# A selective scan whose first four states a unit are weighted and summed by GpSimd before one turn, with B rows in a ring of six quarters

## The reference

```
hidden, gate = split(x @ W_in)                       # 512 channels each
hs   = silu(conv(hidden) + conv_bias)                # 4 taps along the sequence
dt, B, C = split(hs @ W_x, [128, 128 + 16])
dts  = softplus(dt @ W_dt + b_dt)
state[n] = exp(dts * A[n]) * state[n] + dts * B[n] * hs      # 16 states n, 256 steps
y    = (sum over n of C[n] * state[n] + hs * D) * silu(gate)
out  = y @ W_out
```

## Time and profile before

| what | value |
|---|---|
| median of 3 runs | 560.07 us (559.85 to 563.25) |
| profiled execution, its own time | 561.63 us |
| its span | 559.8 us |
| instructions | 10,385 |
| mean granted clock of TensorE | 0.938 of full |
| DMA | 64.16 MB, queue busy 35.9% of 16 engines |

### The profile page before, as it was taken

The page is one execution under the profiler, slowest core; times in us unless marked ns, Lnnn a source line. Parts: engine busy times, 40 slices in busy tenths (PEclk is TensorE's granted clock), DMA queues, the critical chain, the costliest instruction groups (busy, mean ns, idle before and its releaser), DMA issues.

```text
span 559.8 us, 10385 instructions
## 1 busy us (share of the span) xinstructions
PE 497.2 (89%) x3304; PEld 435.6 (78%) x3304; DVE 472.0 (84%) x1053; ACT 365.0 (65%) x877; POOL 318.8 (57%) x465
## 2 busy tenths in 40 slices
PE   4857376868876999999999999999999999999996
PEld 3535264637765988888898998998999999999985
DVE  1399999979999899999999999999889997745451
ACT  2489967578957866689958797974976481350210
POOL 1056669853688677548946676795649443334042
PEclk9798568679996999999999999999999999999999
DMA  7612920003472454021530566436055206553000
GB/s 192 213 63 74 380 76 2 0 0 104 134 260 90 133 177 134 30 76 58 164 120 5 155 190 220 132 89 194 2 161 170 87 15 211 175 164 105 11 11 9
DMA packets 26517, 64.16 MB, mean 115 GB/s; under 512 B 4512, under 2 KB 8352, under 8 KB 26080
## 3 DMA queue, kind: packets, MB, share of 16 engines
q1 hardware_dynamic: 26464, 63.50, 35.9%
HBM read 62.38 MB, written 1.11 MB: 113 GB/s over the span
## 4 chain that ended last, share of the span: by engine, by line
PE 64%; DVE 16%; issue 8%; POOL 5%; ACT 4%; DMA 2%; SPq 0%; DVEq 0%; POOLq 0%; ACTq 0%
PE work L616 40%; PE work L670 13%; PE h_bank L592 6%; DVE acc L1197 5%; POOL dbu L545 4%; DVE st L1181 3%; PE work L592 2%; DVE m L1144 1%; PE h_bank L693 1%; ACT dA L964 1%; DVE wk L1148 1%; DMA b_rows<-b_dram 1%; DVE du L1113 1%; DVE bst L1016 1%; PE work L749 1%
## 5 line engine op out<-in xcount | busy, mean ns | idle before, releaser
L545 POOL TENSOR_TENSOR dbu<-du,b_rows 128x512 f32<-128x512 f32 x128 | 163.4, 1278 | 30.5 <-DVE du L1133 21.0
L964 ACT ACTIVATE dA<-dts,a_neg 128x127 f32<-128x127 f32 x512 | 156.6, 355 | 21.1 <-DVE st L1181 20.0
L1181 DVE TENSOR_TENSOR_SCAN st<-dA,dbu 128x512 f32<-128x512 f32 x128 | 155.1, 1214 | 3.3 <-ACT dA L964 2.7
L592 PE MATMUL h_bank<-ident,st 128*128 128x128 f32 x512 | 85.8, 302 | 32.8 <-DVE acc L1197 21.8
L616 PE MATMUL work<-xsT,stream 128*128 128x128 f32 x896 | 110.0, 278 | 0.8 <-DVE du L1113 0.7
L616 PEld LDWEIGHTS work<-xsT,stream 128*128 128x128 f32 x896 | 105.9, 194 | 2.8 <-DVE du L1113 0.9
L592 PEld LDWEIGHTS h_bank<-ident,st 128*128 128x128 f32 x512 | 66.3, 156 | 47.9 <-DVE st L1181 38.9
L1197 DVE SCALAR_TENSOR_TENSOR acc<-h_bank,c_cols,acc 128x512 f32<-128x512 f32 x128 | 93.2, 728 | 7.4 <-issue 3.4
L567 POOL TENSOR_TENSOR hb<-hb,wbt 128x512 f32<-128x512 f32 (+2 forms) x48 | 55.2, 1153 | 54.0 <-ACT wbt L836 36.3
L491 POOL TENSOR_SCALAR var<-mv 128x1 f32<-128x1 f32 x56 | 13.1, 234 | 83.5 <-DVE mv L1017 83.1
L670 PE MATMUL work<-stream,hb 128*128 128x256 f32 x224 | 53.6, 381 | 0.0
(11 more groups left out here) (157 smaller groups left out, 795.0 us busy)
## 6 DMA issues: line engine op xcount, KB each, us to landing
stream<-in_stream SPq DMA_DIRECT2D x48, 512.0 KB, 3.8
stream<-in_stream SPq DMA_DIRECT2D x48, 384.0 KB, 3.8
b_rows<-b_dram SPq DMA_DIRECT2D x32, 256.0 KB, 4.5
wg<-in_wg SPq DMA_DIRECT2D x1, 1280.0 KB, 7.7
wu<-in_wu SPq DMA_DIRECT2D x1, 1280.0 KB, 10.3
wd<-in_wd SPq DMA_DIRECT2D x1, 1280.0 KB, 12.9
xT<-in_xT SPq DMA_DIRECT2D x4, 256.0 KB, 4.2
out<-row SPq DMA_DIRECT2D x8, 128.0 KB, 2.1
```

Of the source, the lines that this page charges most:

```text
L545: gp.tensor_tensor(tile, du[:, batch % 2, :, lo:hi], b_rows[:, b % 2, k:k + 1, :].to_broadcast([P, ET, P]), ALU.mult).then_inc(s["dbu_read ...
L592: return nc.tensor.transpose(dst, src, ident[:, :])
L964: last = A(dA[i % DA_RING][:, t, 1:P], dts[:, batch % 2, t, lo + 1:hi], ACT.Exp, scale=a_neg[:, t, k:k + 1])
L1181: V.tensor_tensor_scan(st[:, i % ST_RING].rearrange("p t l -> p (t l)"), dA[i % DA_RING].rearrange("p t l -> p (t l)"), dbu[:, i % DBU_RIN ...
```

## The change

- The first EARLY = 4 states of a unit aren't turned one by one. ScalarE writes skip * hs to a tile `early` (four scaled copies, 128x128 each). GpSimd multiplies each of the first four states by its row of C, spread over the partitions (c_rows), into `weighted`, and adds it to `early`. It does so at its scan steps 4 to 7: the weighting ahead of the B product of that step, the addition behind it. A scan tile of these states is free once it is weighted (`taken`).
- TensorE turns states 4 to 15 and, one step later than the last of them, `early` as a sum. ScalarE reads the first of these banks into acc with the scale C[4]; VectorE adds states 5 to 15 as before, and the sum by a plain addition. skip_diag and its products are gone.
- Rows 16 to 19 of b_t (the first four of C) are stored to DRAM with those of B, and spread_c reads them back, one more transfer of 256 KB a unit.
- b_rows is a ring of six quarters (4 states each), and each transfer waits for its own quarter; the SP string orders them one by one among the stream chunks.
- A new load part 7 holds batch 0 of ctxT, wqT, wkT and gam and stands third; the rest of ctxT stays in part 4.
- sq shares the tile of tf, with a wait for the product that read it.
- All ORDER strings and BANK are new. ORDER's parts below are the first lines of three of them.

```diff
 DA_RING, DBU_RING, ST_RING = 2, 4, 4
+B_RING = 6
+EARLY = 4
...
-        "s": [... for step in [("skip", g, 0)] + [("scan", g, k) for k in range(N + LAG)]],
+        "s": [... for step in [("skip", g, 0)] + [("scan", g, k) for k in range(N + LAG + 1)]],
-        "l": [("load", part, 0) for part in range(7)],
+        "l": [("load", part, 0) for part in (0, 1, 7, 2, 3, 4, 5, 6)],
-        "r": [("spread", u, 0) for u in range(U)],
+        "r": [("spread", u, k) for u in range(U) for k in (0, B_PARTS, *range(1, B_PARTS))],
...
     "pe": [
-        "ppappappppsmpsssppssspssssssssmsssssmmssaaaaaaaaaaaaasassmspppssssmmsssmssaspsssmmmmppfssfmmmssmsfffsfsspsfmmf",
+        "ppapppapppmpppmssssssspsssssspppssaaaaaaaaaaaaasasassmmmsssssssssssssmmssmsmmmmpssssppmmmsssssssspssaaaaaaaaaa",
...
     "dve": [
-        "ppaaaaappappppsspssaasssssasasasassssssaassssssssssmmmmmssmsssssssmmppppppmpasmsssmssssffmmmmmsffaaassmafffaas",
+        "ppaaappppppssspsaasasaasasaassaaasssssasssasaaassssaasaasssammmmmassssmssssmmsmsssmssspppppppsmsassasaasassasss",
...
     "pool": [
-        "ssssssssssssssspppppppppppppssssssssmmmsssssssssmmsssspssssssmmmsmmmmmmssssssmmfffffffssssmmmsppppppfffmmfffhs",
+        "ssssssssssssspppppppppppppsssssssssssshmmmssssssmmssssssmmmpsssssssmmssmmmmssssssssssssssssmmsppppppsmmmssmmsm",
...
             def spread_b(u, i):
                 b, lt = divmod(u, LT)
                 n, q = N // B_PARTS, B_PARTS * u + i
                 if i == 0:
                     sp.wait_ge(b_stored[b % 2], 16 * LT * (b // 2 + 1))
+                if q >= B_RING:
+                    sp.wait_ge(s["dbu_ready"], n * (q - B_RING + 1))
+                src = b_dram[b, lt, i * n:(i + 1) * n, :].partition_broadcast(P)
+                sp.dma_start(b_rows[:, q % B_RING], src).then_inc(b_loaded[q % B_RING], 16)
+            def spread_c(u):
+                b, lt = divmod(u, LT)
+                sp.wait_ge(b_stored[b % 2], 16 * LT * (b // 2 + 1))
+                if u >= 2:
+                    sp.wait_ge(s["taken"], EARLY * (u - 1))
+                sp.dma_start(c_rows[:, u % 2], b_dram[b, lt, N:N + EARLY, :].partition_broadcast(P))
...
-            for t in range(ET):
-                last = gp.tensor_scalar(skip_diag[:, t, :], ident[:, :], skip[:, t:t + 1], None, ALU.mult)
...
+                    n = k - ST_RING
+                    if 0 <= n < EARLY:
+                        if n == 0:
+                            pool.wait_ge(c_loaded[b % 2], 16 * (b // 2 + 1))
+                        if b or n:
+                            pool.wait_ge(s["summed"], EARLY * b + n)
+                        if hands_on(b):
+                            pool.wait_ge(s["carry_ready"], hands.index(b) * N + n + 1)
+                        gp.tensor_tensor(weighted[:, :, :], st[:, (i - ST_RING) % ST_RING],
+                                         c_rows[:, b % 2, n:n + 1, :].to_broadcast([P, ET, P]), ALU.mult)\
+                            .then_inc(s["taken"], 1)
...
+                if stage == "scan" and 0 <= k - ST_RING < EARLY:
+                    n = k - ST_RING
+                    pool.wait_ge(s["taken"], EARLY * b + n + 1)
+                    if n == 0:
+                        pool.wait_ge(s["skipped"], b + 1)
+                    gp.tensor_tensor(early[:, :, :], early[:, :, :], weighted[:, :, :], ALU.add).then_inc(s["summed"], 1)
...
+            def turn_sum(g):
+                pe.wait_ge(s["summed"], EARLY * (g + 1))
+                for j in range(widths[g]):
+                    t = claim_h(turned_at[g, N, j])
                     for e in range(ET):
+                        last = transpose(t[:, e * P:(e + 1) * P], early[:, e, j * P:(j + 1) * P])
...
-                if stage == "scan" and 0 < k <= N:
+                if stage == "scan" and EARLY < k <= N:
                     turn_state(b, k - 1)
+                if stage == "scan" and k == N + 1:
+                    turn_sum(b)
...
                 if stage == "skip":
+                    batch, (lo, hi) = GROUPS[b][0], columns(b)
+                    if b == 0:
+                        act.wait_ge(loaded[3], part_size[3])
+                    else:
+                        act.wait_ge(s["h_full"], turned_at[b - 1, N, 0] + 1)
+                    act.wait_ge(s["hs_ready"], batch + 1)
+                    for t in range(ET):
+                        last = A(early[:, t, :], hs[:, batch % 2, t, lo:hi], ACT.Copy, scale=skip[:, t:t + 1])
+                    last.then_inc(s["skipped"], 1)
+                if stage == "scan" and k == EARLY + LAG:
...
                         act.wait_ge(s["h_full"], at + 1)
+                        A(acc[:, u % ACC_RING, :], h_bank[at % H_BANKS][:, :], ACT.Copy,
+                          scale=c_cols[:, batch % 2, u % LT, EARLY:EARLY + 1]).then_inc(s["first_read"], 1)
...
                         if i >= ST_RING:
                             before, n = divmod(i - ST_RING, N)
+                            if n < EARLY:
+                                dve.wait_ge(s["taken"], EARLY * before + n + 1)
+                            else:
+                                dve.wait_ge(s["h_full"], turned_at[before, n, widths[before] - 1] + 1)
...
-                    if k >= LAG:
-                        n = k - LAG
+                    n = k - LAG
+                    if n > EARLY:
...
+                            if n < N:
+                                last = V.scalar_tensor_tensor(out=sums, in0=turned_state, in1=sums, op0=ALU.mult,
+                                                              scalar=c_cols[:, batch % 2, u % LT, n:n + 1], op1=ALU.add)
+                            else:
+                                last = V.tensor_tensor(sums, turned_state, sums, ALU.add)
```

More of the change, by code:

```diff
@@ L76, in chains @@
         "p": [("pre", b, k) for b in range(B) for k in range(PRE_STEPS)],
-        "s": [step for g in range(len(GROUPS)) for step in [("skip", g, 0)] + [("scan", g, k) for k in range(N + LAG)]],
+        "s": [step for g in range(len(GROUPS)) for step in [("skip", g, 0)] + [("scan", g, k) for k in range(N + LAG + 1)]],
         "a": [("adj", b, k) for b in range(B) for k in range(ADJ_STEPS)],
@@ L251, in decoder @@
         b_t = sb("b_t", [2 * N, 2, L])
-        b_rows = sb("b_rows", [P, 2, N, P])
+        b_rows = sb("b_rows", [P, B_RING, N // B_PARTS, P])
         dbu = sb("dbu", [P, DBU_RING, ET, P])
@@ L256, in decoder @@
         carry = sb("carry", [P, N, ET])
-        skip_diag = sb("skip_diag", [P, ET, P])
+        c_rows = sb("c_rows", [P, 2, EARLY, P])
+        early = sb("early", [P, ET, P])
+        weighted = sb("weighted", [P, ET, P])
         c_cols = sb("c_cols", [P, 2, LT, N])
@@ L330, in decoder @@
         work_read = [sem(f"work_read{i}") for i in range(WORK)]
-        b_loaded = [[sem(f"b_loaded{i}_{j}") for j in range(B_PARTS)] for i in range(2)]
+        b_loaded = [sem(f"b_loaded{i}") for i in range(B_RING)]
+        c_loaded = [sem(f"c_loaded{i}") for i in range(2)]
         b_stored = [sem(f"b_stored{i}") for i in range(2)]
@@ L391, in decoder @@
         widths = [w for _, _, w in GROUPS]
-        turned = [(g, n, j) for g in range(len(GROUPS)) for n in range(-1, N) for j in range(widths[g])]
+        turned = [(g, n, j) for g in range(len(GROUPS)) for n in range(EARLY, N + 1) for j in range(widths[g])]
         turned_at = {key: i for i, key in enumerate(turned)}
-        accs = {key: i + 1 for i, key in enumerate(key for key in turned if key[1] >= 0)}
-        skips = {key[::2]: i + 1 for i, key in enumerate(key for key in turned if key[1] < 0)}
+        accs = {key: i + 1 for i, key in enumerate(key for key in turned if key[1] > EARLY)}
+        firsts = {key[::2]: i + 1 for i, key in enumerate(key for key in turned if key[1] == EARLY)}
         def first_unit(g):
@@ L438, in spread_b @@
                 if u >= 2:
-                    sp.wait_ge(s["dbu_ready"], states(u - 2))
-                for i in range(B_PARTS):
-                    n = N // B_PARTS
-                    src = b_dram[b, lt, i * n:(i + 1) * n, :].partition_broadcast(P)
-                    sp.dma_start(b_rows[:, u % 2, i * n:(i + 1) * n, :], src).then_inc(b_loaded[u % 2][i], 16)
+                    sp.wait_ge(s["taken"], EARLY * (u - 1))
+                sp.dma_start(c_rows[:, u % 2], b_dram[b, lt, N:N + EARLY, :].partition_broadcast(P))\
+                    .then_inc(c_loaded[u % 2], 16)
             def store_b(b):
@@ L685, in claim_h @@
                 return h_bank[i % H_BANKS]
-            def turn_skip(g):
-                b, first, w = GROUPS[g]
-                for j in range(w):
-                    t = claim_h(turned_at[g, -1, j])
-                    lt = first + j
+            def turn_sum(g):
+                pe.wait_ge(s["summed"], EARLY * (g + 1))
+                for j in range(widths[g]):
+                    t = claim_h(turned_at[g, N, j])
                     for e in range(ET):
```

(5 more changed lines are left out.)

133 lines of the change are left out of this document (66 added, 67 removed).

## The result

The changed kernel takes 576.7 us (median of three runs, 575.7 to 577.6) where the kernel before takes 560.1: a ratio of 1.028, interval 1.023 to 1.033. Its profiled execution has a span of 575.6 us against 559.8, so 15.8 us are to be found. The forecast was 557.0, with a range that ends at 570. It was wrong, and on the wrong side.

The account below looks back on a forecast made before the run. VectorE was taken to bound the time up to a decisive turn, TensorE's ordered work the rest: 199.5 us work ahead, 32.6 lag, 317.3 behind, 3 lost and 5 tail gave 557.4, forecast as 557 us, range 545 to 570.

Parts of the forecast that it names:

- Two stretches: Whole span: VectorE leads first; TensorE then works off what is left, from about 245 us in the kernel before.
- x5 turn: TensorE's transpose of x5 for unit 0's second experts, forecast as decisive: 199.5 us of VectorE work ahead, 317.3 of TensorE behind.
- work ahead on VectorE + lag: Time of the decisive turn: 199.5 us of VectorE work plus 32.6 us by which VectorE lags its own work.
- TensorE's and VectorE's savings: Fewer turns save 17.5 us on TensorE; fewer sums save 20.5 us on VectorE, mostly where VectorE leads.
- Removed work counts only if other work doesn't move ahead of the decisive turn, and it does.: New orders draw top-k rounds forward (11.3 us by unit 3, state 4), so the gain is 5.5 us, not 17.
- Behind 317.3: After the decisive turn: 317.3 us of TensorE work, 3 us lost instead of 5, and a tail of 5.
- GpSimd becomes the bound: Slower rival, at unit 3, state 4: GpSimd's added work brings the point 12 us later, 569 us; chance 0.21.
- Saving arrives: Faster rival: VectorE reaches the decisive point with lag 27 and TensorE loses no time, 549 us; chance 0.27.
- The signs: Trace marks set beforehand for right, fast or slow: instruction counts, GpSimd's busy time, scan 53's start, dbu and b_rows waits.
- Blocked port: Rival: GpSimd's wide operations hold up VectorE's two-input operations, 1.5 to 5 us more, 559 to 562 us; chance 0.10.
- ScalarE's copies: 32 scaled 128x128 copies on ScalarE, taken at 0.3 us each, 5 to 10 us in all, hidden.
- B rows, taken 0: Loading B rows by quarters with C rows, 8 more transfers: bounds -5 to +3 us, taken as 0.

Follow-up runs that it names:

- e17: Kernel before in the new order strings with states 0 to 3 neither turned nor summed, skip turned ahead of state 4, nothing added: 598.3 us, ratio 1.068.
- e9: Kernel before in its old order strings with states 0 to 3 scanned but neither turned nor summed, nothing added: 551.5 us, ratio 0.984.
- e2: Changed kernel in its new orders with GpSimd's 64 weighting and adding operations cut from 128x512 to 128x4: 577.3 us, ratio 1.028 to the kernel before.
- e3: Changed kernel with memsets of the full tiles in place of GpSimd's weighting and adding operations: 576.0 us, ratio 1.025 to the kernel before.
- e7: Changed kernel with GpSimd's 64 operations cut to 128x4 and ScalarE's 32 copies to one column each: 578.5 us, ratio 1.032 to the kernel before.
- e12: Changed kernel, whole, with ScalarE's first read of the unit moved behind the dA of its step: 576.5 us, ratio 1.029 to the kernel before.
- e16: Changed kernel with GpSimd's added operations cut to 128x4, ScalarE's first read behind dA and the early tile doubled: 575.4 us, ratio 1.023 to the kernel before.
- e5: Changed scheme in the old order strings (SP's string new), GpSimd's 64 added operations cut to 128x4: 576.1 us, ratio 1.026 to the kernel before.
- e11: Changed scheme, old orders, GpSimd's added operations cut to 128x4, ScalarE's first read behind dA, early tile doubled: 566.3 us, ratio 1.009 to the kernel before.

## Why the prediction was wrong, step by step

- **Two stretches, and the x5 turn as the point between.** Half right. As a mark the turn is better than I used it. Every kernel with the old scheme, and every one in the new orders but e17, has a rest of 335.5 to 338.8 us behind that turn. What failed is "the moment at which VectorE releases the decisive turn": TensorE comes to this turn from 15.3 us of unbroken work of its own, after idling 78.9 us where it had idled 54.2. The sum "work ahead on VectorE + lag" has no term for TensorE's own idle time and order up to there.
- **TensorE's and VectorE's savings** (17.5 and 20.5 us). By busy time 14.9 for TensorE, and for VectorE 17.5 in e9, but 12.9 in e2 (459.1) and 3.7 in the changed kernel (468.3). The last step, 9.2 us, comes with the width of GpSimd's operations alone (e2 to the changed kernel), beside which some of VectorE's take longer (below).
- **"Removed work counts only if other work doesn't move ahead of the decisive turn, and it does."** Right in kind: 12.1 us of top-k are drawn ahead. The forecast had the x5 turn at 199.5 + 32.6 = 232.1; it came at 236.8. So 4.7 us of the error lie ahead of the turn. I had put it together from VectorE's work and lag, and the trace doesn't part it into those two terms, since VectorE didn't release the turn.
- **"Behind 317.3; TensorE's lost time 3 instead of 5; tail 5."** This is the step that failed most: 325.3 forecast, 338.8 measured. TensorE is busy 324.3 us behind the turn, 7.0 more than the prices gave. The remaining 14.5 are a tail of 5.0 (the last matmul ends at 570.6) and 9.5 of lost time, where I had put 3. The reason for the 3, that VectorE has slack from there, named only one engine that TensorE waits for: it waits there for ScalarE's xsT (2.9 us, 6 times), VectorE's acc (2.3) and GpSimd's sg (1.5). I had also not held the same sum against the kernel before: it has 337.7 us behind this turn, and a forecast of 12 less had nothing to show for it but 71 instructions fewer (2351 for 2422), some 8 us at 0.11.
- **GpSimd, lag and the rivals.** "GpSimd becomes the bound" was given 569, the nearest in time, for a reason that didn't occur: its sign, VectorE waiting for dbu above 10 us, is 0.3 us in the changed kernel up to 240 us, and e2 takes all of the added work away for nothing. In the old orders it would have been right, and larger. "Saving arrives" is wrong for these orders; e9 shows that 551.5 is what the saving gives when nothing is added for it.
- **The signs.** Nearly all signs of being right came: 416 instructions in TensorE's h_bank group (384 and 32), 88 sums and 8 additions, GpSimd at 396.5 us, 153 fewer TensorE instructions in the first 180 us, 40 instead of 28 MAX8 on wk there. Scan 53 starts at about 182. No sign for the slow side did: dbu waits 0.3 us, GpSimd 86% busy from 40 to 180 us, 1.8 us of waits for b_rows. Only "TensorE packed to the end" failed. So the signs tested whether the change does what it says, and hardly whether the forecast holds.
- **Blocked port.** Right in direction. The Trainium skill (SBUF — State Buffer, "Who interferes with whom") says that a VectorE operation in a two-port mode, or with two SBUF inputs against a GpSimd operation that reads SBUF, and that GpSimd operation exclude each other: the one that starts first holds the ports to its end, and the other waits. tf's scaling (TENSOR_SCALAR 128x256) in e2 and in the changed kernel, where only the width of GpSimd's operations differs:

```profile
L1296 DVE TENSOR_SCALAR tf<-tf 128x256 f32<-128x256 f32 x8 | 2.3, 285 | 0.0
```

```profile
L1296 DVE TENSOR_SCALAR tf<-tf 128x256 f32<-128x256 f32 x8 | 4.4, 552 | 0.0
```

  The rows agree, with 9.2 us of VectorE's busy time in all, and none of it in the time: e2 and the changed kernel end alike. With memsets, which read nothing (e3), the scan o<-tf,sisg with both inputs in SBUF is at 412 ns as in e2, but the product sisg<-tf,sisg stays at 532 ns as in the changed kernel (533; 421 in e2), so the added reads don't explain every row.
- **The start.** Forecast 1.5 us sooner, it is 1.7 (first scan at 36.3). **ScalarE's copies** took 0.386 us each, but they overlap: 10.2 us busy for 32, or 0.32 each, by the measure in which a dA instruction has 0.31. The 0.3 was right.
- **B rows, taken 0.** Borne out: the two added groups take 81.8 us, the four skip_diag operations (2.4 us) are gone, and GpSimd's growth of 77.7 us leaves room for nothing else. Its longest wait for b_rows is 1.8 us.

What stays open: which displaced step of the new strings costs how much. The runs show that the new strings put the x5 turn at 236 to 241 us whatever of the scheme is taken out (e2, e3, e7, e12, e16, e17). The old strings put it at 227.6 for the same code as e2 (e5), but then the rest is 9.8 us longer and the time the same: with GpSimd free, what remains of the scheme costs in the old strings what the new strings cost in theirs. The three top-k rounds ahead of x5's row don't hold the turn, by the trace. What part the rest of the rounds drawn ahead has, what TensorE's 23.5 us of waits for hs, and what ScalarE's dA instructions ahead of wbt, wasn't tried alone. Nor were the 15 us between e11 and e9 parted (on ScalarE 1.3 us of copies a unit and a read of 0.7 where one read of 0.6 stood, on GpSimd 64 operations of 0.2 us, the changed loads and row transfers, one step more between a unit's last state and its output; the sums on VectorE are 96 in both). And the whole old scheme in the new strings wasn't run; e17 stands in for it.

## What to carry to other kernels

Find an instruction near which the bound passes from one group of engines to another, and split each trace there: the time ahead and the rest are two experiments in one. Look also at what it waited for: here TensorE came to it without a wait, so no sum over VectorE alone could say when. Before forecasting a shorter rest, put the same sum to the kernel before. A share in the chain that ended last is no price: 17% for GpSimd was worth nothing in these orders, and the same operations 43 us in the old ones. Choose signs that would come out differently under the rivals. When a change brings both a scheme and an order, measure the four corners, and add the saving with nothing added to it, which shows what can be had at best.

## What the runs showed of the hardware that I had not expected

A ScalarE copy with a scale is mostly fixed cost: 128 columns in the changed kernel, one column in e7.

```profile
L979 ACT ACTIVATE early<-hs,skip x32: 384/386/403, 17.1 to 404.0; 128x128 f32<-128x128 f32 x32
```

```profile
L981 ACT ACTIVATE early<-hs,skip x32: 277/279/296, 17.7 to 401.4; 128x1 f32<-128x1 f32 x32
```

So e7 took away only 3.4 of the copies' 10.2 us. VectorE's large scans kept a mean of 1.21 to 1.22 us in every run, however busy GpSimd was, while the small ones did not: o<-tf,sisg, 128x128 with both inputs in SBUF, took 412 ns in e2 and 649 in the changed kernel. The order counts as well: the kernel before, which has none of the added operations, has 548.
